# Spreading the last set's rows over the partitions, and moving loads and joins, in a four-layer spectral kernel

## The reference

```python
xs = rfft2(x)                                   # (B, H, W//2+1, 8, 48)
o1 = relu(xs * w1 + b1)                         # complex, block by block
o2 = o1 * w2 + b2
x = irfft2(softshrink(o2, 0.01)) + x
```

## Time and profile before

| | |
|---|---|
| median of 3 runs | 1030.41 us (1029.93 to 1033.44) |
| the profiled execution, its own time | 1035.22 us |
| its span, first to last instruction | 1033.4 us |
| PE busy | 925.4 us, 90% |
| DVE, ACT, POOL busy | 56%, 46%, 8% |
| mean granted PE clock | 0.960 of full |
| PE's waits of over 5 us | 16.0 (the first `Bm`), 5.1 at 65 us, 13.8 at 423 us, 21.2 at 987 us |
| moved by DMA | 184.39 MB, mean 178 GB/s |

### The profile page before, as it was taken

The page is one execution under the profiler, slowest core; times in us unless marked ns, Lnnn a source line. Parts: engine busy times, 40 slices in busy tenths (PEclk is TensorE's granted clock), DMA queues, the critical chain, the costliest instruction groups (busy, mean ns, idle before and its releaser), DMA issues.

```text
span 1033.4 us, 14264 instructions
## 1 busy us (share of the span) xinstructions
PE 925.4 (90%) x5168; PEld 466.4 (45%) x5168; DVE 574.3 (56%) x869; ACT 476.5 (46%) x757; POOL 80.7 (8%) x157
## 2 busy tenths in 40 slices
PE   3879999999999989499999999999999999999812
PEld 1536556665766646144444434443433434344301
DVE  1245554454544847476775676665667656656411
ACT  1435445545544424133343445655565655556501
POOL 3011111111111100000000110000000000000001
PEclk8889999999999999799999999999999999999966
DMA  8976699478658696934333443442754566451464
GB/s 277 328 204 187 249 286 356 136 201 293 224 159 281 197 313 166 210 90 123 96 105 89 128 128 106 103 131 77 237 138 138 159 211 177 137 204 49 130 127 184
DMA packets 94255, 184.39 MB, mean 178 GB/s; under 512 B 12455, under 2 KB 72129, under 8 KB 92394
## 3 DMA queue, kind: packets, MB, share of 16 engines
q1 hardware_dynamic: 84362, 142.33, 47.1%
q0 software_dynamic: 9824, 41.14, 12.1%
HBM read 104.29 MB, written 79.14 MB: 177 GB/s over the span
## 4 chain that ended last, share of the span: by engine, by line
PE 79%; DMA 10%; DVE 4%; issue 3%; ACT 2%; SPq 1%; DVEq 0%; POOL 0%; ACTq 0%; POOLq 0%
PE psum L910 16%; PE psum L901 16%; PE psum L940 9%; PE psum L889 6%; PE psum L977 6%; PE psum L993 6%; PE psum L1017 6%; PE psum L920 5%; PE psum L951 4%; DMA RX<-rows_along_w 4%; PE psum L1004 3%; DMA RG<-rows_along_h 3%; PE psum L866 2%; DMA RX<-spectrum 1%; ACT RA L1174 1%
## 5 line engine op out<-in xcount | busy, mean ns | idle before, releaser
L1318 DVE SCALAR_TENSOR_TENSOR RA<-psum,RA 112x896 f32<-112x896 f32 (+1 forms) x120 | 124.3, 1036 | 221.6 <-ACT RA L1174 221.4
L1174 ACT ACTIVATE RA<-psum,small 112x896 f32<-112x896 f32 (+1 forms) x120 | 115.9, 966 | 96.8 <-PE psum L910 94.3
L910 PE MATMUL psum<-RA,RW 112*64 112x448 f32 (+1 forms) x640 | 132.4, 535 | 1.4 <-ACT RA L1165 1.4
L1165 ACT ACTIVATE RA<-psum,RW 112x448 f32<-112x448 f32 (+1 forms) x160 | 89.4, 610 | 79.3 <-PE psum L901 79.3
L940 PE MATMUL psum<-RD,const 128*128 128x384 f32 (+1 forms) x304 | 100.0, 450 | 9.9 <-DVE RA L1278 5.3
L1278 DVE COPY RD<-psum 128x672 f32<-128x672 f32 (+2 forms) x122 | 69.7, 572 | 67.0 <-PE psum L940 60.7
L1159 ACT ACTIVATE RA<-psum 128x384 f32<-128x384 f32 (+2 forms) x72 | 50.6, 704 | 86.5 <-PE psum L889 59.1
L889 PE MATMUL psum<-const,RX 128*112 128x128 f32 x528 | 71.0, 289 | 21.1 <-DMA RX<-rows_along_w 21.1
L1159 ACT ACTIVATE RD<-psum 128x384 f32<-128x384 f32 (+2 forms) x122 | 64.1, 526 | 39.6 <-PE psum L940 37.8
L1303 DVE TENSOR_TENSOR RX<-RX,RA 112x768 f32<-112x768 f32 (+2 forms) x80 | 80.7, 1009 | 1.5
L889 PEld LDWEIGHTS psum<-const,RX 128*112 128x112 f32 x528 | 63.6, 186 | 39.7 <-issue 33.2
(11 more groups left out here) (102 smaller groups left out, 1092.7 us busy)
## 6 DMA issues: line engine op xcount, KB each, us to landing
RG<-rows_along_h SPq DMA_DIRECT2D x7, 3072.0 KB, 11.7
rows_along_h<-RD SPq DMA_DIRECT2D x96, 144.0 KB, 2.9
RX<-x SPq DMA_DIRECT2D x16, 768.0 KB, 8.0
out<-RA POOLq DMA_DIRECT2D x16, 768.0 KB, 4.5
rows_along_w<-RX SPq DMA_DIRECT2D x54, 224.0 KB, 5.3
rows_along_h<-RD SPq DMA_DIRECT2D x64, 168.0 KB, 3.1
RX<-rows_along_w SPq DMA_DIRECT2D x12, 672.0 KB, 6.8
spectrum<-RA POOLq DMA_DIRECT2D x48, 168.0 KB, 5.1
```

The costliest lines, as they stand in the source:

```text
L910: mm = nc.tensor.matmul(bank[b * HALF:(b + 1) * HALF, a * BANK:a * BANK + nk * H], w4[layer][0:ROWS, g, b, a], hidden(slot)[0:ROWS, b * N: ...
L1165: done = nc.scalar.activation(hidden(slot)[0:ROWS, b * N:b * N + nk * H], banks(key)[0:ROWS, b, 0:nk * H], ACT.Relu, bias=bias[layer][0:RO ...
L1174: nc.scalar.activation(dst, src, ACT.Relu, bias=minus_lambda_l0 if key[0] == "S4" else minus_lambda).then_inc(act_emptied, 1)
L1318: nc.vector.scalar_tensor_tensor(out=dst, in0=src, scalar=LAMBDA / 64 if key[0] == "S4" else LAMBDA, in1=dst, op0=ALU.add, op1=ALU.min).th ...
```

## The change

**Start:** only two of the four x loads of pass 1 are issued before the rounds, the other two in rounds 0 and 1. The operands of layer 1's folding are loaded in rounds 4 and 5, `fwd_c` in round 18; the folding itself is done four rounds later (DVE in steps 6 to 11, PR in round 14).

**Stage B:** `load_y(4)` is issued right behind `load_y(3)`, and item z then loads y(z + 5) in place of y(z + 4).

**Stage C, joins:** `join` leaves its place between `shrink` and `add_to` of 4L2 and goes behind `add_to` of 4L3, so behind the copy of 6C too. It joins the same step in the same round.

**End:** the inverse of pass 2 runs two units in each round instead of one (rounds 38 to 41). The rows of the last pass are placed by `SPREAD`, which gives a group every eighth row and one or two sparser series, over all four quarters; `inv_w_spread` has the rows of the matrix in the same order. A group is stored in one transfer for each series and quarter (8 or 12 in place of 4) and loaded by itself, by one transfer for each series, as soon as it is stored. Of the last group's 8 stores ACT issues 4. The last load brings the 24 rows of group 4 in place of the 48 of groups 3 and 4. POOL's hold on the output is gone, and the output of the last pass is stored in 8 halves, the even ones by POOL, the odd ones by SP.

The diff, cut to its core:

```diff
+SPREAD = [[(0, 8), (5, 16)], [(1, 8), (13, 16), (15, 32)], [(2, 8), (6, 16), (31, 32)], [(3, 8), (14, 16)], [(4, 8), (7, 16)]]
...
-PREP_ROUND = 10
+PREP_ROUND = 14
...
+def spread_of(e):
+    pieces, at = [], 0
+    for first, step in SPREAD[e % PASS_GROUPS]:
+        pieces.append((slice(first, HP, step), slice(first, P, step), slice(at, at + HP // step)))
+        at += HP // step
+    return pieces
...
+def inverse_rate(p):
+    return 1 if p < PASSES - 2 else 2
...
-            if 0 <= r - last_inverse_round(p) < S1_UNITS:
-                o += [("6C", p, r - last_inverse_round(p))]
+            if 0 <= r - last_inverse_round(p) < S1_UNITS // inverse_rate(p):
+                o += [("6C", p, inverse_rate(p) * (r - last_inverse_round(p)))]
...
             o += [("TC", r - L3_LAG - 1)]
-    o += [("6C", PASSES - 2, v) for v in range(C_ROUNDS - last_inverse_round(PASSES - 2), S1_UNITS)]
+        if 0 <= r - last_inverse_round(PASSES - 2) < S1_UNITS // 2:
+            o += [("6C", PASSES - 2, 2 * (r - last_inverse_round(PASSES - 2)) + 1)]
...
+            def store_spread(e, xs):
+                p = e // PASS_GROUPS
+                for x in xs:
+                    for rows, _, cols in spread_of(e):
+                        sp.dma_start(rows_along_h[p, x, rows].rearrange("k h c -> h k c"),
+                                     turned(e)[x * HP:(x + 1) * HP, cols]).then_inc(turned_stored[e % TURN_SLOTS], 16)
...
+            def load_spread(e):
+                p = e // PASS_GROUPS
+                if e == LAST_PASS:
                     wait_g_free(p)
+                wait_turned_stored(sp, e)
+                src = rows_along_h[p].rearrange("x k h c -> (x k) h c")
+                for _, rows, _ in spread_of(e):
+                    sp.dma_start(G(p)[rows], src[rows]).then_inc(g_loaded[p % 2], 16)
...
-            for k in range(X_PARTS):
+            for k in range(X_PARTS // 2):
                 load_x(1, k)
-            load_prep("q0", l1_q)
-            load_prep("e0", l1_e)
-            load_prep("t0", l1_t)
-            load_prep("va0", l1_w3)
-            sp.dma_start(fwd_c, fwd_c_dram).then_inc(fwd_loaded, 16)
...
+                if r < X_PARTS // 2:
+                    load_x(1, X_PARTS // 2 + r)
+                if r == 4:
+                    load_prep("q0", l1_q)
+                    load_prep("e0", l1_e)
+                elif r == 5:
+                    load_prep("t0", l1_t)
+                    load_prep("va0", l1_w3)
+                elif r == 18:
+                    sp.dma_start(fwd_c, fwd_c_dram).then_inc(fwd_loaded, 16)
...
-            load_y(3)
+            for m in (3, 4):
+                load_y(m)
...
-                if z + 4 < ITEMS:
-                    load_y(z + 4)
+                if z + 5 < ITEMS:
+                    load_y(z + 5)
...
+                for q in range(PASS_GROUPS - 1):
+                    if r == min(10 * (PASSES - 1) + 7 + 2 * q, C_ROUNDS - 1):
+                        load_spread(LAST_PASS + q)
+            load_spread(2 * ALL_GROUPS - 1)
+            for v in range(1, S1_UNITS, 2):
+                wait_emptied(sp, ("6C", PASSES - 1, v))
+                dst, src = last_out(v)
+                sp.dma_start(dst, src).then_inc(odd_out_stored, 16)
...
-                    if (p, k) == (PASSES - 2, X_PARTS // 2):
-                        pool.wait_ge(g_loaded[(PASSES - 1) % 2], g_uses(2 * PASSES - 1))
...
                     shrink(key, s, 0)
-                    if s + 2 < ALL_STEPS:
-                        join(s + 2)
                     vec.wait_ge(vec_emptied, plan.vec[key])
                     add_to(modes_c(s), s, shrunk(0, step_of(s)[3]), edges_of(s), 0.5)
+                    if s < L3_LAG:
+                        join(s + 2)
                 elif stage == "4L3":
...
                     add_to(modes_c(s), s, shrunk(1, step_of(s)[3]), 0, None)
+                    if s + L3_LAG + 2 < ALL_STEPS:
+                        join(s + L3_LAG + 2)
```

More of the change, by code:

```diff
@@ L222, in constants @@
     kw_order = [0, 32] + list(range(1, 32))
+    spread = np.concatenate([np.arange(HP)[rows] for e in range(PASS_GROUPS) for rows, _, _ in spread_of(e)])
     inv_w = np.zeros((2, Q, W))
@@ L234, in constants @@
             inv_w_flip[j, 32 + k, j] = 2 * sw[k, kw_order]
+    inv_w_spread = inv_w.copy()
+    for half in (0, HP):
+        inv_w_spread[:, half + spread] = inv_w[:, half:half + HP]
     n = np.arange(FOLD + 1)
@@ L521, in wait_turned_stored @@
         def wait_turned_stored(eng, e):
-            eng.wait_ge(turned_stored[e % TURN_SLOTS], 64 * (e // TURN_SLOTS + 1))
+            stores = sum(4 * (1 if n < LAST_PASS else len(spread_of(n))) for n in range(e % TURN_SLOTS, e + 1, TURN_SLOTS))
+            eng.wait_ge(turned_stored[e % TURN_SLOTS], 16 * stores)
         def g_uses(p):
-            return sum(16 * (8 if m == 2 * PASSES - 1 else 1) for m in range(p % 2, p + 1, 2))
+            return sum(16 * (sum(map(len, SPREAD)) if m == 2 * PASSES - 1 else 1) for m in range(p % 2, p + 1, 2))
         def wait_flipped_stored(eng, p, g):
@@ L553, in c_updates @@
                     counts["L3", r - L3_LAG] = k
+                if r + 2 < ALL_STEPS:
+                    k += 1
+                    counts["J", r + 2] = k
             return counts
@@ L567, in stage_views, with last_out @@
                     stage(p, k)[x * HP:(x + 1) * HP].rearrange("q (y r) -> q y r", r=PASS_ROWS))
+        def last_out(v):
+            p, k = PASSES - 1, v // 2
+            return (a.rearrange("p (j v n) -> p j v n", j=2, v=2)[:, :, v % 2] for a in (out[p, k], out_slot(p, k)))
         block = ctx.enter_context(nc.Block())
@@ L617, in load_g @@
                 sp.dma_start(G(p), src).then_inc(g_loaded[p % 2], 16)
-            def load_g_part(p, last):
-                e = PASS_GROUPS * (p + 1) - (2 if last else 4)
-                if not last:
-                    wait_g_free(p)
-                for turn in (e, e + 1):
-                    wait_turned_stored(sp, turn)
-                split = columns_of(PASS_GROUPS * (p + 1) - 2)[0]
-                lo, hi = (split, HP) if last else (0, split)
-                for x in range(4):
-                    sp.dma_start(G(p)[x * HP + lo:x * HP + hi], rows_along_h[p, x, lo:hi]).then_inc(g_loaded[p % 2], 16)
+            def store_spread(e, xs):
[7 more added lines that the diff above has]
+                if e == LAST_PASS:
+                    wait_g_free(p)
+                wait_turned_stored(sp, e)
+                src = rows_along_h[p].rearrange("x k h c -> (x k) h c")
+                for _, rows, _ in spread_of(e):
+                    sp.dma_start(G(p)[rows], src[rows]).then_inc(g_loaded[p % 2], 16)
             for k in range(X_PARTS):
@@ L775, in _ @@
                         wait_emptied(sp, ("5C", e, part))
-                    store_turned(ALL_GROUPS + e)
-                for p in range(PASSES):
-                    if p < PASSES - 1 and r == 10 * p + 15:
-                        load_g(PASSES + p)
-                    elif p == PASSES - 1 and r == 10 * p + 11:
-                        load_g_part(PASSES + p, 0)
-            load_g_part(2 * PASSES - 1, 1)
+                    if ALL_GROUPS + e < LAST_PASS:
+                        store_turned(ALL_GROUPS + e)
+                    else:
+                        store_spread(ALL_GROUPS + e, range(4) if e < ALL_GROUPS - 1 else range(2))
+                for p in range(PASSES - 1):
+                    if r == 10 * p + 15:
+                        load_g(PASSES + p)
+                for q in range(PASS_GROUPS - 1):
[6 more added lines that the diff above has]
+                sp.dma_start(dst, src).then_inc(odd_out_stored, 16)
+            sp.wait_ge(odd_out_stored, 16 * S1_UNITS // 2)
         @block.gpsimd
@@ L841, in _ @@
                     wait_emptied(pool, ("6C", p, 2 * k + 1))
-                    if (p, k) == (PASSES - 2, X_PARTS // 2):
-                        pool.wait_ge(g_loaded[(PASSES - 1) % 2], g_uses(2 * PASSES - 1))
                     pool.dma_start(out[p, k], out_slot(p, k)).then_inc(out_stored[(p * X_PARTS + k) % OUT_SLOTS], 16)
+            for v in range(0, S1_UNITS, 2):
+                wait_emptied(pool, ("6C", PASSES - 1, v))
+                dst, src = last_out(v)
+                pool.dma_start(dst, src).then_inc(out_stored[v // 2 % OUT_SLOTS], 16)
             for s in range(OUT_SLOTS):
@@ L965, in s6c @@
                         dst = bank[to * HALF:(to + 1) * HALF, j * BANK:j * BANK + n].rearrange("p (h c) -> p h c", c=PASS_C)
-                        mm = nc.tensor.matmul(dst, inv_w[rows], G(p)[rows, h:h + 2], start=True, stop=True)
+                        mm = nc.tensor.matmul(dst, matrix[rows], G(p)[rows, h:h + 2], start=True, stop=True)
                 mm.then_inc(filled, 1)
@@ L1207, in _ @@
                     copy(*s5_views(key, 0, at)).then_inc(act_emptied, 1)
+                    if key == ("5C", ALL_GROUPS - 1, 1):
```

(7 more changed lines are left out.)

24 lines of the change are left out of this document (12 added, 12 removed).

## The result

The changed kernel took 996.88 us in the median of 4 runs (993.3 to 1000.97), the kernel before 1030.33 us in the same comparison: a ratio of 0.9662, 95% interval 0.9641 to 0.9683. It is 33.5 us faster. In a later comparison it was 0.9627 (0.9596 to 0.9658). The forecast was 986 with a range of 975 to 1000. The profiled execution took 993.3 us with a span of 991.3; it is the shortest of the four.

What follows compares the result with a forecast made beforehand. The page showed PE busy nine tenths of the span, so gains had to come from its idle stretches. 7.3 + 14.3 + 10 + 13.1 = 44.7 us off the 1030.4 us median gave 985.7, say 986; range 975 to 1000.

Steps and rivals of the forecast that it cites:

- the likeliest case: Whole kernel: all four parts work, 44.7 us gained, 986 us, own range 976 to 997; chance 0.64.
- Start, 7.3: Start: PE's wait for `Bm` group 3 (5.1) and half clock (2.7) go, moved folding costs 0.5; bounds 4 and 8.
- Without 1660 KB ahead and without a choked queue: Start: `Bm` group 3's load then needs under 10 us, so PE's 5.1 us wait ends at nothing.
- fifth rival: Round 18: `fwd_c` stops the queue, the slot reused in round 22 is 9.7 us late; 996 us, chance 0.04.
- Stage B, 14.3: Stage B: earlier y(4) saves PE's 13.8 us wait and 2.0 of half clock, less 1.5; bounds 8 and 15.8.
- second rival: Stage B only trades waits: y(5) or the flipped input ends a new 8 us wait; 994 us, chance 0.12.
- Stage C, 10: Stage C: moved joins end waits of 5C and 3L3; 12.7 us together, 10 taken, bounds 4 and 13.
- SP's update loads wait for it, but they go out five rounds ahead: Stage C: update loads wait for the join, which moves about 4 us later, but go out five rounds ahead.
- third rival: Stage C: joins don't pay, 3L3 waits as before, C gives 1 us; 995 us, chance 0.11.
- End, 13.1: End: 6C units -0.9, last group's store 1, last load 9.5, output 3.5 us gained; bounds 8 and 18.
- fourth rival: End: spread rows load no faster per byte and short runs slow the output; 991 us, chance 0.05.
- Between 0 and -2, take -1: End, last group's store: eight issues in two queues take what four took in one; 1 us gained.

Runs made afterwards that it cites:

- a_same: The changed kernel itself, untouched, measured again as the yardstick beside other runs: 994.31 us, ratio 0.9627.
- x_y: The changed kernel with y loaded one item later again, as in the kernel before: 1014.19 us, ratio 0.9808.
- a_order: The changed kernel with group 3 of the last pass loaded one round later, behind SP's stores of the last group: 995.71 us, ratio 0.9639.
- a_split: The changed kernel with `fwd_c` loaded as 96 rows and 1 row: 993.24 us, ratio 0.9615.
- a_gfirst: The changed kernel with `G`'s load issued ahead of the update loads of its round in stage C: 989.9 us, ratio 0.9579.
- b_split: The kernel before with `fwd_c` alone loaded as 96 rows and 1 row, in its old place: 1027.65 us, ratio 0.9945.
- x_joins: The changed kernel with every join back ahead of the copies: 1002.62 us, ratio 0.9715.
- a_best: The changed kernel with `G` loaded ahead of the update loads, `fwd_c` as 96 rows and 1 row, all eight last-group stores by ACT: 986.04 us, ratio 0.9546.
- a_contig: The changed kernel with the last pass's groups as blocks of neighbouring rows, still stored and loaded group by group: 1020.34 us, ratio 0.9897.

## Why the prediction was right, and where it was not

**Sum and time.** The forecast of the likeliest case held: all four parts work, and the gain from profile to profile was 42.1 us of span where the sum said 44.7. The median came out 10.9 us above 986. Of this, 2.6 are the terms, and that they are so few is in part luck: start, stage B, stage C and tail were forecast at 7.3, 14.3, 9.1 and 14.0 us and measured 6.2, 16.0, 10.5 and 9.5 in the pair of profiles, so two terms that were too low hide most of what the end lacked. The rest comes of one sentence: "so I take the gain from the median". The profiled execution of before lay 4.8 us above its median, that of the changed kernel 3.6 below its own, and the gain of the two executions was carried to the medians. The four runs of the changed kernel have spans of 991.3, 993.5, 996.7 and 999.2 us at mean clocks of 0.976, 0.974, 0.971 and 0.968. From the first to the last, 0.008 of some 995 us is 8 us of clock lost, and the span is 7.9 us longer: in these four the scatter is time at the lower level. It isn't always: of `a_same`'s executions, two have the same mean clock, 0.976, and spans of 989.6 and 993.9 us. One place where such time arises is seen in `x_y`: PE waits 2.38 us for `G` of pass 0, and then works at 1.2 GHz for some 10 us; after the 1.40 us of the changed kernel's profiled execution it did not.

```profile
174.53 2.83 PE L997 MATMUL psum<-const,RG 128*96 128x66 f32 x16 [2.38 <-DMA RG<-rows_along_h]
```

```profile
175.00:180.00 5.00, 5.00 (x23) 0.50 0.35 142
180.00:185.00 5.00, 5.00 (x14) 0.54 0.33 91
```

A second place is the wait for `G` in stage C: behind 2.90 us of it in `a_order` and 2.42 in `x_y`, PE has 3.4 us at 1.2 GHz; behind 2.51 in the changed kernel's profile none. That the slower executions of the changed kernel are those in which one of these waits is long is argued; none of them was profiled. The runs beside it don't single out one of the two: the untouched kernel scatters by 11.3 us (6 runs), `a_split`, with the table split, by 2.6 (4 runs), and `a_gfirst`, with the whole table but no wait for `G` in stage C, by 2.9 (4 runs).

**Start, 7.3.** It measured 6.2 in the pair and 6 to 9 by the experiments. The size was right, the cause was not. "Without 1660 KB ahead and without a choked queue" named two things together and put the weight on the first; `b_split` keeps the bytes ahead and loses that wait, though smaller ones take back more than half of what it was worth. The trace of before had it: `fwd_c`'s packets of 4096 bytes ran for some 16 us, one after another. The Trainium skill, "DMA: Bandwidth & Descriptors", section "Why a DMA increments its semaphore by 16 and not by 1", has the rule by which 97 rows leave one engine; by that page's figures it is an estimated 14 us. The trace agrees with it, in both places where the table was put. The fifth rival's choked queue in round 18 came as described, with 16.15 us, and was covered as the prediction had it; no run shows that it cost anything. The moved folding cost 0.7 us, where 0.5 was taken: in stage A PE waits 2.4 us for ACT's copies into `RX`, and 1.7 before.

**Stage B, 14.3.** It measured 16.0 in the pair, just over the upper bound, and `x_y` gives 17.5. The wait, the half clock and its price were as worked out. The 1.5 us taken off for y(5) and the rest of item 1 was not needed: y(5) is issued at 411.79 us, DVE begins its sums at 428.12 without having waited for it, and PE has no new wait in stage B. So the second rival fell.

**Stage C, 10.** With the 0.9 for the 6C units, 9.1 was forecast, 10.5 measured. Of that the joins are 7 (`x_joins`) and the units -1. Most of the rest belongs to the one execution of before: its stage C has 3.4 us at half clock from 707.5 us on, a loss of 1.7, and 1.1 us of wait for `G`; `b_split`, whose stage C is the same code, has neither, and is 2.7 us shorter there. Some 2 us stay open. The waits named did all go, 11.1 us. What the prediction passed over was in its own sentence "SP's update loads wait for it, but they go out five rounds ahead": true of their data, but `G`'s load stands behind them in the queue, and it is not early. That took 4 to 5 us back, and `a_gfirst` shows it. The third rival, joins that don't pay, fell.

**End, 13.1.** 9.5 in the pair less 1 in stage C. The last load, 6 us, took 6.1, so the fourth rival fell. The output took 13.2 us where 12 was taken, and what lies behind the last byte, which was to stay, fell by 1.2. The step that failed is the store of the last group: "Between 0 and -2, take -1"; its last landing came 10.6 us after the product, against 7.0 before, 3.6 us worse. The prediction counted the eight issues in two queues and did not ask what SP was waiting for when they fell due: the landing of the stores of the group before. It named this very sign as one that would make it wrong: from the group's first issue to its last landing it took 10.0 us, against 6.4 before. `a_best`, which frees the stores of it, gets 2.9 of it back; `a_order` shows that moving it within SP gets some 2, since the last load then runs together with that of group 3.

**Why spreading pays.** "The spread rows are nearer to the full load" was a guess between two rates and hit, but `a_contig` shows what it brought: without it, loading group by group loses 12 to 13 us of tail instead of winning 9 to 10. By the Trainium skill, "DMA: Bandwidth & Descriptors", the same section, a transfer of 12 rows goes to 12 engines and one of 6 rows to 6, always the lowest-numbered ones; four such transfers put four rows on each, with 12 as with 6. That is what the two tails have in common: 48 rows in 15.6 us and 24 rows in 15.0. The packets bear this out: 48 of 24576 bytes before, 3.2 us each, 11 at a time; 24 in `a_contig`, 2.8 us each, 5 at a time, in sets of twelve and of six. (A window of the view counts a packet whole where it starts; hence the 0.89 and 0.93 of before there, with 0.10 in the next.) A spread group has one transfer of 16 rows and one of 8, at most two rows on an engine: 6.1 us.

That rule gives how many rows are under way at once, and not how long one takes: the packets of before and of `a_contig` take up to 3.6 us, those of the spread rows 1.2 to 2.2. The port rule of the Trainium skill, "SBUF — State Buffer", section "Door 1: The DMA port swizzle", fits that if it is taken transfer by transfer, which the prediction did not do: in a transfer of 12 neighbouring rows each port has four rows, in one of 6 one port has four and one two, in a spread one each has two. The prediction's estimate for four rows on a port was 3.6 us, and all packets of before's second and fourth set took 3.6; of `a_contig`'s second set four took some 3.6 and two 2.6. Four such transfers one after another are an estimated 14.4 us. So the gain has two factors, two sets in place of four and shorter packets in each, and both fit. No run varies one without the other: `a_contig` changes the rows' places, their number in a transfer and the number of transfers together.

## What to carry to other kernels

Look at the number of rows of each transfer before its bytes: a table of 97 rows held a queue for some 16 us, wherever it was put, and two transfers in place of one did away with the 5.1 us wait as moving 1660 KB did. Where neighbouring rows are loaded in several small transfers, count the rows of each and see in the packets whether they run one set after another. When a wait is added or moved in front of a queue's entries, list what stands behind them in that queue and when each is due; here it was `G`'s load in one place and the last stores in the other. And when a gain is worked out from one profiled execution, compare its mean clock with that of the other runs before it is set against their median.

## What the runs showed that was not expected

24 neighbouring rows in four transfers of six (576 KB) took as long as 48 in four of twelve (1152 KB): 15.0 and 15.6 us. Two stores of 144 KB issued behind such a load took up to 14.2 us to land; the median of their kind is 3.3 in the changed kernel, and before it was up to 10.2 at the end. Splitting off the one row of 97 shortened the issue of the transfer behind it from 17.45 to 1.61 us and from 16.15 to 3.41 us, while the one row's own took 7.12 and 3.78. Waits of 2.38, 2.42 and 2.90 us in PE were followed by 10, 3.4 and 3.4 us at the lower clock, one of 2.51 us by none.
